# A mixture-of-experts tail: GpSimd's row scatters wait for the next expert's relus, and its DRAINs stand behind experts 3, 6, 9 and 12

## The chip, the cores and the metric

The kernel runs on one core of a Trainium2 chip. The metric is the device time of one execution in microseconds (us), from the first instruction to the last, as the median of several timed runs. Beside the timed runs there is one execution taken by the hardware profiler; its page and trace are what the numbers below come from.

## What is computed

The reference is one transformer block in float32: 8 sequences of 512 tokens with 128 channels. A modulated layer norm feeds attention with 16 heads of 64 channels, whose output is gated and added; then a second modulated layer norm feeds a mixture of 16 experts, and the expert outputs are gated and added again. The change lies in the last part:

```python
score = jax.nn.softmax(xf @ Wg + bg, axis=-1)
gate = jnp.max(score, axis=-1)
idx = jnp.argmax(score, axis=-1)
...
keep = pos < cap                       # cap = 4096 / 16 = 256 rows for each expert
buf = zeros((16, 256, 128)).at[idx, safe_pos].add(where(keep, xf, 0))
h = relu(einsum('ecd,edh->ech', buf, W1) + b1)      # 128 -> 512
y = einsum('ech,ehd->ecd', h, W2) + b2              # 512 -> 128
out = y[idx, safe_pos] * gate
x = x + gb * where(keep, out, 0)
```

## The kernel before

The attention part (8 batches of 8 head pairs, some 780 us of the span) is not touched. At its end GpSimd scatters each token's row (normed input, residual, gate times `gb`, token number: 385 floats) into a DRAM buffer `xbuf` at its expert's place (`scatter`, line 487).

Then the 16 experts follow, each with 256 rows, written out by hand on every engine:

- TensorE, for expert e: `hidden` (line 1270), 12 matmuls into four PSUM banks, three for each bank, with a semaphore step `hm` behind each bank; then the transposes of the next expert's rows (`turn_e`, line 1261); then `down` (line 1295), 16 matmuls that wait bank by bank for the relus (`hr`), with a step `ym` behind each half of 128 rows.
- ScalarE: four relus of 128x256 (line 837), each behind its `hm` and each giving one step of `hr`, which therefore stands at 4(e + 1) when expert e's relus are done. Behind them the high half of the next rows (line 828) and of the weights of the expert after (line 808).
- VectorE: the low halves (lines 1807 and 1773), and `output` (lines 1819 to 1825): token numbers to integers (`yi`), then three operations that add the bias, multiply by the gate and add the residual, with a step of `y` for each half. `output(e - 1)` runs in turn e of the loop up to e = 9 (`LAGGING`); experts 9 to 13 are put out in their own turn, 14 and 15 by halves after the loop.
- SyncE: a load queue; rows of expert e + 5 when `y` says that expert e is out, and weights of expert e + 8 when `ym` says so.
- GpSimd: `expert(e, r)` (line 567): it waits for `yi` and `y`, and starts two indirect DMAs (line 572), a and b below, that write 128 rows each to their tokens' places in the output. The results lie in four buffers `ye`, used in turn, so `output(e)` waits until expert e - 4 has landed (`ysc0` to `ysc3`). A DRAIN stands behind expert 11 and behind the last one (line 580).

The end of the kernel is GpSimd's wait for all four `ysc` semaphores.

Of the kernel before, what the change touches and what calls it, by code (L numbers as in the profile page):

```python
# [44 lines left out]
E, FF = 16, 512  # L45
CAP = B * S // E
NB = FF // P
# [27 lines left out]
def program(nc, x_d, xt_d, wall_d, wv_d, cols_d, wo_d, bo_d, wg_d, bg_d, w1_d, w2_d, b2_d, wmod_d,  # L75
            consts_d, ktab_d, iota_d, out_d):
    ctx = ExitStack()
    with ctx:
# [3 lines left out]
        def sem(name):  # L82
            return ctx.enter_context(nc.semaphore(name))
# [113 lines left out]
        s = {n: sem("s_" + n) for n in names}  # L197
# [177 lines left out]
        def _(gp):  # L375
# [191 lines left out]

            def expert(e, r):
                gp.wait_ge(s["yi"], e + 1)
                for t in range(ST):  # L570
                    gp.wait_ge(s["y"], ST * e + t + 1)
                    gp.indirect_dma_start(out=out_d.rearrange("b s d -> (b s) d"),
                                          out_offset=bass.IndirectOffsetOnAxis(ap=yidx[:, r, t:t + 1], axis=0),
                                          in_=ye[r][:, t, :], in_offset=None,
                                          bounds_check=last_token, oob_is_err=False).then_inc(s[f"ysc{r}"], 16)

            for e in range(E):
                expert(e, e % 4)
                if e in (11, E - 1):
                    gp.drain()  # L580
            for r in range(4):
                gp.wait_ge(s[f"ysc{r}"], 16 * ST * E // 4)
# [1328 lines left out]
```

## Time and profile before

| what | us |
|---|---|
| timed runs: median of 3 | 863.76 |
| timed runs: lowest, highest | 863.61, 4828.07 |
| the profiled execution, its own time | 870.51 |
| its span, first to last instruction | 868.6 |
| TensorE busy (share of the span) | 853.3 (98%) |
| GpSimd busy (share of the span) | 544.7 (63%) |

Stretches and start times below are counted from the span's start. The median stands 6.75 us under the profiled execution's own time. One of the three timed runs took over 4.8 ms; the profile is of an execution without that.

### The profile page before, as it was taken

The page shows a single profiled execution, that of the slowest core. Times are in us where ns is not written, and L with a number is a line of the kernel's source. Part 1 is how long each engine was busy: PE and PEld are TensorE (multiplying, and loading weights), DVE is VectorE, ACT ScalarE, POOL GpSimd, SP SyncE. Part 2 cuts the span into 40 slices and gives each one's busy share as a digit, 9 for nine tenths or more (in the row PEclk, how much of TensorE's full clock was granted, in tenths as well). Part 3 has the DMA queues.
Part 4 walks back from the last instruction along what each step waited for, and adds up shares of the span by engine and source line. Part 5 has one row for each costly group of instructions (what it writes and reads, how often), then busy time and mean ns, then how long its engine had stood idle before and what let it go on. Part 6 is the DMA issues. An engine that isn't in the chain of part 4 may idle for free.

```text
span 868.6 us, 17491 instructions
## 1 busy us (share of the span) xinstructions
PE 853.3 (98%) x5531; PEld 680.2 (78%) x5531; DVE 657.2 (76%) x2041; ACT 724.0 (83%) x2012; POOL 544.7 (63%) x807
## 2 busy tenths in 40 slices
PE   8999999999999999999999999999999999999996
PEld 5777877778877788777787777877778877777985
DVE  6778778777878688777878787877878777876564
ACT  5888888988889888888988889888988888884653
POOL 5856466666576764776567755766667656663454
PEclk9999999999999999999999999999999999999998
DMA  8000970000000100000000000000000000016960
GB/s 295 2 1 2 264 197 14 14 19 20 14 13 1 37 2 13 14 20 18 14 13 9 20 14 13 1 21 2 13 14 13 11 14 13 2 35 191 311 204 23
DMA packets 25611, 41.40 MB, mean 48 GB/s; under 512 B 3334, under 2 KB 17527, under 8 KB 25136
## 3 DMA queue, kind: packets, MB, share of 16 engines
q1 hardware_dynamic: 21872, 33.60, 12.8%
q0 software_dynamic: 3072, 5.94, 1.9%
q8 instruction: 45, 0.74, 0.4%
q10 hardware_dynamic: 576, 0.75, 0.3%
q14 instruction: 46, 0.38, 0.1%
HBM read 25.93 MB, written 16.82 MB: 49 GB/s over the span
## 4 chain that ended last, share of the span: by engine, by line
PE 96%; DVE 2%; ACT 1%; issue 1%; DMA 0%; POOL 0%; POOLq 0%; another core or an unknown queue 0%; DVEq 0%
PE bank L988 23%; PE bank L1021 17%; PE bank L941 17%; PE bank L1001 16%; PE bank L1028 5%; PE bank L968 5%; PE bank L1295 4%; PE bank L985 3%; PE bank L1270 3%; PE bank L961 0%; ACT prob L690 0%; DMA x<-in_x 0%; PE bank L1036 0%; PE bank L891 0%; PE bank L1261 0%
## 5 line engine op out<-in xcount | busy, mean ns | idle before, releaser
L501 POOL TENSOR_SCALAR prob<-prob,rsum 128x128 f32<-128x128 f32 x508 | 261.2, 532 | 220.7 <-DVE rsum L1447 215.5
L690 ACT ACTIVATE prob<-srow,nmax 128x512 f32<-128x512 f32 (+3 forms) x512 | 285.9, 559 | 57.7 <-DVE nmax L1435 56.2
L1435 DVE CUSTOM_DVE_ANT_0 srow<-bank,consts 128x512 f32<-128x512 f32 (+3 forms) x512 | 247.0, 489 | 54.0 <-issue 40.3
L1001 PE MATMUL bank<-consts,prob 128*128 128x128 f32 x1280 | 201.8, 272 | 0.3 <-ACT pt L699 0.3
L1001 PEld LDWEIGHTS bank<-consts,prob 128*128 128x128 f32 x1280 | 158.2, 141 | 23.6 <-ACT pt L699 1.2
L699 ACT ACTIVATE pt<-bank 128x384 f32<-128x384 f32 x318 | 157.0, 498 | 11.3 <-PE bank L1001 11.1
L1452 DVE SCALAR_TENSOR_TENSOR qx<-bank,qbias,consts 128x512 f32<-128x512 f32 x128 | 96.0, 750 | 72.1 <-PE bank L941 65.3
L1021 PE MATMUL bank<-pt,v 128*64 128x512 f32 x1008 | 149.6, 439 | 0.6 <-issue 0.6
L988 PE MATMUL bank<-khi,qhi 128*128 128x512 f32 (+2 forms) x384 | 141.4, 368 | 0.5 <-issue 0.2
L494 POOL TENSOR_TENSOR qlo<-qx,qhi 128x384 fp32r<-128x384 f32 x127 | 128.4, 1011 | 12.4 <-ACT qhi L653 5.7
L988 PE MATMUL bank<-khi,qlo 128*128 128x512 f32 (+2 forms) x384 | 130.3, 339 | 0.0
L988 PE MATMUL bank<-klo,qhi 128*128 128x512 f32 (+2 forms) x384 | 129.0, 336 | 0.0
L1021 PEld LDWEIGHTS bank<-pt,v 128*64 128x64 f32 x1008 | 67.6, 136 | 75.8 <-issue 60.1
L1459 DVE SCALAR_TENSOR_TENSOR klo<-bank,khi 64x512 fp32r<-64x512 f32 x128 | 87.9, 687 | 31.6 <-ACT kx L648 29.5
L690 ACT ACTIVATION_READ_ACCUMULATOR prob<-srow,nmax 128x1 f32 x512 | 97.4, 190 | 0.0
L941 PE MATMUL bank<-hhi,whi 128*128 128x512 f32 x177 | 85.8, 485 | 0.0
L653 ACT ACTIVATE qhi<-qx 128x384 fp32r<-128x384 f32 x128 | 66.3, 518 | 23.3 <-DVE qx L1452 22.0
L988 PEld LDWEIGHTS bank<-khi,qhi 128*128 128x128 f32 x384 | 72.4, 189 | 14.5 <-issue 2.6
L988 PEld LDWEIGHTS bank<-klo,qhi 128*128 128x128 f32 x384 | 72.7, 189 | 10.9 <-issue 0.5
L647 ACT ACTIVATE khi<-bank 64x512 fp32r<-64x512 f32 x128 | 75.1, 587 | 2.1 <-PE bank L908 0.5
L988 PEld LDWEIGHTS bank<-khi,qlo 128*128 128x128 f32 x384 | 72.1, 188 | 5.1
L941 PE MATMUL bank<-hlo,whi 128*128 128x512 f32 x177 | 69.9, 395 | 0.0
(262 smaller groups left out, 1422.8 us busy)
## 6 DMA issues: line engine op xcount, KB each, us to landing
xbuf<-fill SPq DMA_DIRECT2D x4, 1540.0 KB, 23.7
x<-xbuf SPq DMA_DIRECT2D x13, 385.0 KB
raw<-in_w SPq DMA_DIRECT2D x16, 256.0 KB
prob<-in_w SPq DMA_DIRECT2D x16, 256.0 KB
h2T<-in_xt SPq DMA_DIRECT2D x8, 256.0 KB, 2.9
out<-row SPq DMA_DIRECT2D x8, 256.0 KB, 2.4
x<-in_x SPq DMA_DIRECT2D x1, 1536.0 KB, 11.4
modb<-mod_rows SPq DMA_DIRECT2D x1, 1536.0 KB, 7.2
```

The lines of the kernel that those rows point to most:

```text
L494: gp.tensor_tensor(qlo[:, h, :], qx[:, h, P:S], qhi[:, h, :], ALU.subtract).then_inc(s["ql"], 1)
L501: end = gp.tensor_scalar(part, part, rsum[:, par, 4 * h + q:4 * h + q + 1], 1.0, ALU.mult, ALU.mult)
L647: act.activation(khi[0:HD, h, :], source[h * HD:(h + 1) * HD, :], ACT.Copy, scale=C_QKV)
L690: act.activation(prob[:, par, h, QOFF[q]:QOFF[q] + P * (q + 1)], srow[:, k % 4, 0:P * (q + 1)], ACT.Exp, bias=nmax[:, par, k:k + 1], scale ...
L699: act.activation(pt[:, h, KOFF[g]:KOFF[g] + GW[g]], source[:, 0:GW[g]], ACT.Copy)\
L941: last = pe.matmul(out, w[:, a, cols], h, start=(i == 0), stop=(i == 2))
L988: last = pe.matmul(out, a[:, h, (q - 1) * P:q * P], b[:, h, 0:P * (q + 1)], start=(i == 0), stop=(i == 2))
L1001: last = pe.transpose(out[:, n * P:(n + 1) * P], prob[:, par, h, QOFF[q] + k * P:QOFF[q] + (k + 1) * P], ident)
L1021: last = pe.matmul(otb[h * HD:(h + 1) * HD, k * P:S], v[:, g, k, at + h * HD:at + (h + 1) * HD], pt[:, h, KOFF[k]:KOFF[k] + S - k * P], st ...
L1435: dve.tensor_tensor_reduce(out=srow[:, k % 4, 0:w], in0=scb[k % 2][:, 0:w], in1=mask[:, S - w:S], scale=-1.0, scalar=BIG, op0=ALU.add, op1 ...
L1452: dve.scalar_tensor_tensor(qx[:, h, :], prb[h][:, :], qbias[:, h, a:a + 1], qtab, ALU.add, ALU.mult).then_inc(s["qe"], 1)
L1459: dve.scalar_tensor_tensor(klo[0:HD, h, :], source[h * HD:(h + 1) * HD, :], C_QKV, khi[0:HD, h, :], ALU.mult, ALU.subtract).then_inc(s["kl ...
```

## The change

GpSimd waits for one more semaphore value before it scatters expert e, for e from 0 to 13: `hr` at 4(e + 2), which is reached when the four relus of expert e + 1 are done. And the DRAINs, which stood behind experts 11 and 15, stand behind 3, 6, 9, 12 and 15.

```diff
             def expert(e, r):
                 gp.wait_ge(s["yi"], e + 1)
+                if e + 2 < E:
+                    gp.wait_ge(s["hr"], NB * (e + 2))
                 for t in range(ST):
                     gp.wait_ge(s["y"], ST * e + t + 1)
                     gp.indirect_dma_start(out=out_d.rearrange("b s d -> (b s) d"),
...
             for e in range(E):
                 expert(e, e % 4)
-                if e in (11, E - 1):
+                if e in (3, 6, 9, 12, E - 1):
                     gp.drain()
```

No instruction of another engine changes. On GpSimd, at experts 13, 14 and 15 and the end of the program, the order before is (`row` and `xh` hold the results, `yidx` the token numbers; a line's waits are the semaphores it needs):

```order
L572 DMA out<-row,yidx 4096x128 [waits s_y,s_yi]
L572 DMA out<-row,yidx 4096x128 [waits s_y]
L572 DMA out<-xh,yidx 4096x128 [waits s_y,s_yi]
L572 DMA out<-xh,yidx 4096x128 [waits s_y]
L572 DMA out<-xh,yidx 4096x128 [waits s_y,s_yi]
L572 DMA out<-xh,yidx 4096x128 [waits s_y]
L78 UNCONDITIONAL_BRANCH [waits s_ysc2,s_ysc3,s_ysc1,s_ysc0]
```

The same place after the change, where the scatter stands on line 574:

```order
L574 DMA out<-row,yidx 4096x128 [waits s_y,s_hr,s_yi]
L574 DMA out<-row,yidx 4096x128 [waits s_y]
L574 DMA out<-xh,yidx 4096x128 [waits s_y,s_yi]
L574 DMA out<-xh,yidx 4096x128 [waits s_y]
L574 DMA out<-xh,yidx 4096x128 [waits s_y,s_yi]
L574 DMA out<-xh,yidx 4096x128 [waits s_y]
L78 UNCONDITIONAL_BRANCH [waits s_ysc2,s_ysc3,s_ysc1,s_ysc0]
```

Nothing has changed its place; expert 13 is the last with the new wait, and experts 14 and 15 have none. The DRAINs, which such a listing does not print, stand as the diff says.

## Rows read from the trace of the kernel before

**Rows 1.** The page: busy time by engine, and the chain that ended last.

```profile
PE 853.3 (98%) x5531; PEld 680.2 (78%) x5531; DVE 657.2 (76%) x2041; ACT 724.0 (83%) x2012; POOL 544.7 (63%) x807
...
PE 96%; DVE 2%; ACT 1%; issue 1%; DMA 0%; POOL 0%; POOLq 0%; another core or an unknown queue 0%; DVEq 0%
```

**Rows 2.** The chain that ended last, in order of time: start us, us, what.

```profile
852.77 1.42 PE bank L1270 x12
...
856.20 1.42 PE bank L1270 x12
...
860.02 2.34 PE bank L1295 x10
...
862.38 0.30 DVE xh L1822
...
863.33 0.02 issue
863.36 0.02 POOLq L571
863.37 0.73 issue
864.10 0.97 POOL out L572
```

**Rows 3.** Timeline of ACT: start us, us, line, operation, [idle before, releaser].

```profile
836.75 1.57 ACT L837 ACTIVATE srow<-bank,smallT 128x256 f32<-128x256 f32 x4 [1.35 <-PE bank L1270]
...
840.15 0.84 ACT L837 ACTIVATE srow<-bank,smallT 128x256 f32<-128x256 f32 x2 [1.04 <-issue]
841.84 0.47 ACT L837 ACTIVATE srow<-bank,smallT 128x256 f32<-128x256 f32 x1 [0.85 <-PE bank L1270]
843.27 0.47 ACT L837 ACTIVATE srow<-bank,smallT 128x256 f32<-128x256 f32 x1 [0.95 <-remote]
...
849.74 1.57 ACT L837 ACTIVATE srow<-bank,smallT 128x256 f32<-128x256 f32 x4 [1.04 <-PE bank L1270]
...
853.17 1.57 ACT L837 ACTIVATE srow<-bank,smallT 128x256 f32<-128x256 f32 x4 [1.07 <-PE bank L1270]
...
857.25 1.26 ACT L837 ACTIVATE srow<-bank,smallT 128x256 f32<-128x256 f32 x3 [2.24 <-PE bank L1270]
859.49 0.47 ACT L837 ACTIVATE srow<-bank,smallT 128x256 f32<-128x256 f32 x1 [0.98 <-remote]
```

**Rows 4.** Timeline of POOL, scatters of experts 3, 6, 8, 11, 12 and 15.

```profile
820.53 0.97 POOL L572 DMA_INDIRECT out<-xh,yidx  x1 [0.30 <-issue]
822.88 0.97 POOL L572 DMA_INDIRECT out<-row,yidx  x1 [1.38 <-DVE row L1825]
...
831.50 0.97 POOL L572 DMA_INDIRECT out<-xh,yidx  x1 [0.30 <-issue]
...
837.52 0.97 POOL L572 DMA_INDIRECT out<-row,yidx  x1 [1.39 <-DVE yidx L1819]
...
843.90 0.97 POOL L572 DMA_INDIRECT out<-xh,yidx  x1 [0.30 <-issue]
...
849.75 0.97 POOL L572 DMA_INDIRECT out<-xh,yidx  x1 [0.30 <-issue]
853.65 0.97 POOL L572 DMA_INDIRECT out<-row,yidx  x1 [2.92 <-DVE yidx L1819]
...
860.09 0.97 POOL L572 DMA_INDIRECT out<-xh,yidx  x1 [0.30 <-issue]
...
865.37 0.97 POOL L572 DMA_INDIRECT out<-xh,yidx  x1 [0.30 <-issue]
```

**Rows 5.** Timeline of DVE: the last operation of experts 9 and 12.

```profile
838.31 0.42 DVE L1825 TENSOR_TENSOR row<-row,x 128x256 f32<-128x256 f32 x1
...
850.39 0.43 DVE L1825 TENSOR_TENSOR row<-row,x 128x256 f32<-128x256 f32 x1
```

**Rows 6.** Line 580, the DRAINs: count, ns shortest/median/longest.

```profile
L580 POOLq DRAIN  x2: 3621/3871/4121, 848.7 to 864.4; - x2
```

## The prediction

> **What bounds the kernel now.** I read the page first, then the chain that ended last, then the timelines of the engines that the chain passes through. TensorE is busy 98% of the span and makes up 96% of the chain; GpSimd is busy 63%, and the chain knows it only at its end [rows 1]. So most of what GpSimd does is free, and the change touches only the last 60 us of a span of 868.6. There the chain [rows 2] goes through TensorE from expert to expert: the hidden layer of expert 14 starts at 852.77 and that of expert 15 at 856.20, which makes 3.43 us for an expert that nothing delays. The last expert does not keep to that: its second layer is still running at 862.36, VectorE takes the result at 862.38, and GpSimd's wait is over at 863.36, its scatter a begins 0.73 later at 864.10, scatter b at 865.37, and the span ends at 868.6.
>
> By the pace of 3.43 us, expert 15's second layer would be done at 856.20 + 3.43 = 859.63, so it is 2.73 us late. ScalarE's timeline shows where [rows 3]: in experts 10, 13 and 14 the four relus take 1.57 us in one piece, and that of expert 14 starts 0.40 after the hidden layer; in expert 15 they start 1.05 after it (857.25), and the fourth comes after 0.98 us of idle time. Expert 11 shows the same: two relus at 840.15, then gaps of 0.85 and 0.95, so that the fourth starts at 843.27 in place of 840.15 + 1.57 - 0.47 = 841.25, 2.02 late. These are the only two such places among the relus. What they share is seen on GpSimd [rows 4]: both lie in a train of six scatters with 0.30 us between them, 8a to 10b from 837.52 to 843.90 + 0.97 = 844.87, and 12a to 14b from 853.65 to 860.09 + 0.97 = 861.06. Elsewhere the scatters of this part come in pairs with more than 1 us before each pair. That a train holds up TensorE's completions, on which the relus wait, is thus a coincidence of two places, not a thing that a row shows by itself, and the chances below reflect it. The second train exists because of the DRAIN behind expert 11: y of expert 12 was ready at 850.39 + 0.43 = 850.82 [rows 5], but its scatter began at 853.65.
>
> **The change, part by part.** *The new waits.* `output(e - 1)` stands behind `low_x(e + 1)` on VectorE, which needs ScalarE's operation behind the relus of e; so for experts 0 to 8 the new value of `hr` is always there before `y`. For expert 9 it is close: the relus of expert 10 end at 836.75 + 1.57 = 838.32 [rows 3] and y comes at 838.31 + 0.42 = 838.73 [rows 5]. Ten of the fourteen waits cost 0 and move nothing. Expert 10 would wait for the relus of 11, which end at 843.27 + 0.47 = 843.74, but it stands behind a new DRAIN anyway. Expert 12 waits for the relus of 13: 849.74 + 1.57 = 851.31; expert 13 for those of 14: 853.17 + 1.57 = 854.74 [rows 3]. Behind the waiting instruction stand only later scatters; what waits for those is `output(e + 4)` through `ysc`, and the end.
>
> *The DRAINs.* A DRAIN took 3.6 to 4.1 us from its issue [rows 6], but it is issued while the scatters before it still run. Its price on GpSimd is the gap that it makes: from the end of 11b, 849.75 + 0.97 = 850.72, to 12a at 853.65 is 2.93 us, against 0.30 in a train [rows 4], so at most 2.63 each. Below, the bound is 0, where y comes later than the DRAIN ends. I take the whole gap of 2.93, since the one measured case is this very place. By the Trainium skill, Perfetto Trace Analysis, section "DMA Instruction — SWDGE (GPSIMD)", the end that the profiler gives is the point at which the last core has written its descriptors; by that reading alone a DRAIN behind it would have nothing to wait for, expert 15's scatter would not be held by GpSimd at all, and the sum below would gain 2.73 in place of 1.76. The gap of 2.93 does not agree with so short a DRAIN.
>
> The schedule of GpSimd from this, with 1.276 from scatter to scatter ((843.90 - 837.52) / 5, [rows 4]):
> - Behind 3: 3b ends at 820.53 + 0.97 = 821.50, so 4a comes at 824.43 in place of 822.88. It has 1 us and more of slack in each of the next pairs, and is back on time at expert 6. Cost 0.
> - Behind 6: 6b ends at 832.47, so 7a at 835.40, 7b, 8a, 8b, 9a without a break, and 9b at 841.78, ending 842.75. Expert 7 came before in a pair of its own: this is again a train of six, beside the relus of expert 11.
> - Behind 9: 10a at 845.68 in place of 842.62, 10b at 846.96, ending before 11a is due. Here the train of before is cut.
> - 11 as before; no DRAIN, so 12a comes 0.75 behind the relus of 13: 852.06, 12b ends at 854.31.
> - Behind 12: 13a at 857.24, 13b, 14a, 14b at 861.07, ending 862.04; 15a at 862.34, 15b at 863.61.
> Buffers: the scatters of 9 start at latest at 841.78 and those of 10 at 846.96, and VectorE needs their buffers for experts 13 and 14, whose turns come after 851 us; a landing takes at most 868.6 - 865.37 = 3.2 us. Cost 0.
>
> *The sum.* While expert 15's hidden layer and relus run (856.20 to 858.2), GpSimd is now inside the DRAIN for the first half, and the train of four has just begun. I take it that the 2.73 us of delay goes. Then the wait of scatter 15a is over at 863.36 - 2.73 = 860.63, and 15a could start at 861.37; but GpSimd is only free for it at 862.34. What is late next is GpSimd's own queue: 15a moves from 864.10 to 862.34, a gain of 1.76 us, and the rest of the end moves with it. In the middle I count nothing, since the train beside expert 11 is moved and not removed. Span 868.6 - 1.76 = 866.8; own time 870.51 - 1.76 = 868.75. The median of the runs shown stands 6.75 under the profiled time, so 863.76 - 1.76 = 862.0 us.
>
> **The rivals.** *Both stalls go: 860.0.* If what matters is not the length of a train but a scatter that starts beside certain relus, the wait for `hr` cures expert 11 too. For it: 10a moves by 3 us, away from those relus. Against: 8a to 9b stay beside them, only later by 0.43. It would give 2.02 more, 862.0 - 2.0 = 860.0.
>
> *No effect: 863.8.* The stalls do not come from the scatters, or exist only in the profiled execution, which took 6.75 us more than the timed ones. For it: no row names GpSimd as what the relus waited for; two of the gaps have an unknown releaser [rows 3]. Then 15a waits for y at 863.36 as before, and the train ends in time at 862.04. The change would do nothing that it says for ten of fourteen experts anyway.
>
> *Slower: 865.8, by longer trains in front of a late queue.* The place is 7a to 9b: six scatters from 835.40, with a DRAIN at both ends, beside the relus of experts 10 and 11. If a train holds TensorE from its third scatter on, both experts are hit, at 2.02 each where it was one. From then on everything is later by 2.0 us and the end keeps its own stall, since 13a to 14b is still a train of four beside the second layer of expert 15: 863.76 + 2.02 = 865.8. It decides from the point at which a stall shows on the relus of expert 10. Against: before, the first three scatters of each train left the relus alone.
>
> *The median is a disturbed execution.* One timed run took 4828.07 us; were two of three like that, the result would be in milliseconds. No row tells what happened there, and DRAINs could make it rarer or more frequent.
>
> **How the numbers follow.** Forecast, end gain alone: 0.38. Both stalls go: 0.14. No effect: 0.29. Slower by new trains: 0.16. Disturbed median: 0.03. The predicted time is 862.0. The range has to reach to the bounds: at the low side both stalls gone and a little left over, 859.5; at the high side the slower case with 0.2 more for the distance between two medians, 866.0. The two sides leave out the disturbed case and the tails. A difference of 2% is 17 us, about what a measurement of this kernel can tell from no change: all cases but the last lie well within it, and I keep 0.01 for faster and 0.04 for slower.
>
> **What would show it right or wrong.** Right: a gap near 2.9 us on GpSimd behind experts 3, 6, 9 and 12; scatters of 0 to 9 where neither a DRAIN nor a train moves them at the same distance from y; the fourth relu of expert 15 without a gap; 15a directly behind 14b, with an idle time of 0.30, near 862.3. A stall still at the relus of expert 11. Wrong: gaps among the relus of expert 15 with GpSimd inside its DRAIN (then trains are not the cause), a DRAIN that takes 5 us behind three experts' scatters (then 15a is late by itself), or a span that changes in the attention part, which the change does not touch.

## The result, and the profile after

The changed kernel takes 868.57 us (median of 5 runs, 868.28 to 868.72), the kernel before 863.76 beside it. The ratio of the undisturbed runs is 1.0054, with a 95% interval from 1.0041 to 1.0066: slower by 4.8 us, inside 2%, and outside the range of 859.5 to 866.0. The odd part is that the profile says the reverse: its span is 866.7 us after and 868.6 before. Both are true, and how they can be is the main finding of this study.

The page of the changed kernel, as [rows 1]: busy time, then the chain that ended last.

```profile
PE 850.2 (98%) x5531; PEld 678.7 (78%) x5531; DVE 657.1 (76%) x2041; ACT 723.5 (83%) x2012; POOL 545.5 (63%) x807
...
PE 7%; issue 1%; POOL 1%; DVE 0%; POOLq 0%; ACT 0%; DVEq 0%
```

TensorE has hardly changed its share of busy time, but the chain has: before, TensorE made up 96% of it; now the chain can be followed back only to 774.51, and the shares above add up to 9% of the span. Its last stretch, as [rows 2] (start us, us, what):

```profile
852.22 0.30 issue
852.52 0.97 POOL out L574
853.49 0.30 issue
853.80 0.97 POOL out L574
854.77 1.59 issue
856.36 0.04 POOLq L573
856.40 0.73 issue
857.14 0.29 POOL out L574
```

TensorE, ScalarE and VectorE are not in it any more: from 847.42 to the end it is GpSimd's scatters and DRAINs one behind the other. The timeline of GpSimd, as [rows 4]: behind each DRAIN, the end of the scatters before it and the start of those after it, and the last four.

```profile
820.37 0.97 POOL L574 DMA_INDIRECT out<-xh,yidx  x1 [0.30 <-issue]
825.78 0.97 POOL L574 DMA_INDIRECT out<-row,yidx  x1 [4.44 <-ACT srow L839]
...
832.28 1.17 POOL L574 DMA_INDIRECT out<-xh,yidx  x1 [0.30 <-DVE xh L1827]
837.31 0.97 POOL L574 DMA_INDIRECT out<-xh,yidx  x1 [3.86 <-ACT srow L839]
...
844.23 0.97 POOL L574 DMA_INDIRECT out<-row,yidx  x1 [0.30 <-issue]
847.42 0.97 POOL L574 DMA_INDIRECT out<-xh,yidx  x1 [2.21 <-ACT srow L839]
...
853.80 0.97 POOL L574 DMA_INDIRECT out<-row,yidx  x1 [0.30 <-issue]
857.14 0.97 POOL L574 DMA_INDIRECT out<-row,yidx  x1 [2.37 <-DVE xh L1827]
...
859.69 0.97 POOL L574 DMA_INDIRECT out<-xh,yidx  x1 [0.30 <-issue]
860.96 0.97 POOL L574 DMA_INDIRECT out<-xh,yidx  x1 [0.30 <-issue]
862.24 0.97 POOL L574 DMA_INDIRECT out<-xh,yidx  x1 [0.30 <-issue]
863.52 0.97 POOL L574 DMA_INDIRECT out<-xh,yidx  x1 [0.30 <-issue]
```

Four gaps of 4.44, 3.86, 2.21 and 2.37 us stand behind experts 3, 6, 9 and 12; between them the scatters come in full trains, 4a to 6b, 7a to 9b, 10a to 12b and 13a to 15b. Two things are to be read with care. The releaser "ACT srow" is only one of the semaphores that the instruction needs: the DRAINs in front ended at 824.96, 836.49, 846.60 and 856.32, each 0.82 us before the scatter, and e2 below shows that the relus cost nothing. And GpSimd is 63% busy over the whole span, as before, while it has, but for the DRAINs, no free slot in the last 40 us.

The relus of experts 13, 14 and 15 on ScalarE, as [rows 3]:

```profile
845.45 1.57 ACT L839 ACTIVATE srow<-bank,smallT 128x256 f32<-128x256 f32 x4 [1.07 <-PE bank L1272]
...
848.88 1.57 ACT L839 ACTIVATE srow<-bank,smallT 128x256 f32<-128x256 f32 x4 [1.07 <-PE bank L1272]
...
852.30 1.57 ACT L839 ACTIVATE srow<-bank,smallT 128x256 f32<-128x256 f32 x4 [1.59 <-PE bank L1272]
```

They are 3.43 us apart and in one piece, from expert 3 to the last. VectorE is done with expert 15 at 855.99 + 0.29 = 856.28 and the scatters that it feeds start at 862.24, 6 us later. The DRAINs, as [rows 6]:

```profile
L582 POOLq DRAIN  x5: 5608/6618/6948, 819.3 to 859.4; - x5
```

They last 5.6 to 6.9 us from their issue, while the scatters before them still run; what they cost GpSimd is the gap.

### The profile page after: what moved, and what is told of

It reads as the page before. It is cut to its first block and busy times, and to the rows that moved or that the text cites. A ratio compares the mean times of both kernels' runs of the same rounds, so it can differ in the third digit from the quotient of the medians.

```text
span 866.7 us, 17494 instructions
## 1 busy us (share of the span) xinstructions
PE 850.2 (98%) x5531; PEld 678.7 (78%) x5531; DVE 657.1 (76%) x2041; ACT 723.5 (83%) x2012; POOL 545.5 (63%) x807
```

## The experiments

They ran on several chips, and the kernel before, which ran beside each, shows two kinds: on two chips it takes 863.8 to 863.9 us (e1 to e4; e17 and e18), on three others 870.4 to 871.8 us (e5 to e8; e9 to e12; e13 to e16). The two do not overlap: no timed run of it on the first two took over 866.93, none on the other three under 869.62. I call them quiet and stalling. Each chip was used at one time only, so it is not shown whether the difference belongs to the chip or to the time. Every ratio below is against the kernel before on the same chip. The edits shown for e2, e3 and e4 are made to the changed kernel, all others to the kernel before.

**e1: the kernel before again, quiet chip.** No edit.

> The kernel before, unchanged, to see whether its stalls on the relus of experts 11 and 15 are a property of it. Theory Q (the scatter queue of GpSimd is the bound of the changed tail; the profile of before was of an execution with stalls that the timed ones lack): time 863.8, span of the profile near 861.9, each expert 3.43 us apart on ScalarE from expert 3 to 15, no gap among the relus of 11 and 15, the last relus starting near 852.3. Theory S (trains of scatters hold up TensorE, in every run): stalls of 0.9 to 2 us at experts 11 and 15 again, span near 868.6.

Measured: 863.62 us, span 861.4, ratio 0.9996 [0.9986, 1.0006]. Relus of expert 15 and the scatters from 11b on:

```profile
852.09 1.57 ACT L837 ACTIVATE srow<-bank,smallT 128x256 f32<-128x256 f32 x4 [1.58 <-PE bank L1270]
```

```profile
845.29 0.97 POOL L572 DMA_INDIRECT out<-xh,yidx  x1 [0.31 <-issue]
849.18 0.97 POOL L572 DMA_INDIRECT out<-row,yidx  x1 [2.92 <-DVE yidx L1819]
...
856.89 0.97 POOL L572 DMA_INDIRECT out<-xh,yidx  x1 [0.30 <-issue]
858.16 0.97 POOL L572 DMA_INDIRECT out<-xh,yidx  x1 [0.30 <-issue]
```

No stall. The profiled execution that the prediction read (870.51) thus looks like one of a stalling chip, and the timed median beside it (863.76) like one of a quiet chip; that is inferred from the times and the stalls, since their chips are not known. And here the scatter queue sets the end already before the change: the halves of y of expert 15 are ready at 855.17 and 856.06, but 12a to 15b run as one train from 849.18, and 15b starts at 858.16. After the change 15b starts at 863.52, 5.4 later; the spans differ by 866.7 - 861.4 = 5.3.

**e2: the new waits alone (quiet).**

```diff
-                if e in (3, 6, 9, 12, E - 1):
+                if e in (11, E - 1):
```

> The new waits for the relus, the DRAIN left behind expert 11 alone. Theory Q: the waits are met or cost under 0.5 us each on a queue that has slack again, 863.8 to 864.5. Rival W (the waits cost the time, as the profile of after names ScalarE's relus as the releaser of nearly every pair): 866 or more, most of the 4.8 us.

Measured: 864.01, ratio 1.0005 [0.9995, 1.0014]. The waits for the relus cost nothing that these runs can tell, and by the interval at most 1.2 us. Rival W falls, although the profile names the relus for 21.2 us of GpSimd's waits in the changed kernel.

**e3: the DRAINs alone (quiet).**

```diff
-                if e + 2 < E:
-                    gp.wait_ge(s["hr"], NB * (e + 2))
```

> DRAINs behind 3, 6, 9, 12 and 15, without the new waits. Theory Q: all of the 4.8 us, 868.0 to 868.7, with scatters without a break from the one behind 12 to the end. Rival W: 864 to 866.

Measured: 869.47, ratio 1.0059 [1.0045, 1.0073], the same as the change (1.0054). The whole loss is in the DRAINs. One of its six runs took 2169.91 us, so DRAINs behind 3, 6, 9 and 12 do not exclude the long executions.

**e4: the change without its DRAIN behind 12 (quiet).**

```diff
-                if e in (3, 6, 9, 12, E - 1):
+                if e in (3, 6, 9, E - 1):
```

> The change without its DRAIN behind expert 12 (3, 6, 9 and 15 left). Theory Q: the queue is full from 9 on and loses one gap of 2.4 less 0.3, so 2.1 us less than the change: 866.5. If the queue were not the bound: 868.6 as the change.

Measured: 866.98, ratio 1.0033 [1.0022, 1.0045]. It gives back 1.6 of the 4.8 us, against 2.1 expected; in the profile 15b starts at 861.79, 1.73 before that of the change, though its relus of expert 15 come 0.31 later (852.61 against 852.30), which makes 2.04. So the queue part is as expected. Of the rest, 0.3 us is there from the start of the program (TensorE's first output projection begins at 42.38 against 42.09), and 0.25 is in the last DRAIN, which ends 0.53 us behind the last landing in place of 0.28 (see e17).

**e5 and, on other chips, e10, e14 and e17: no DRAIN behind 11.**

```diff
-                if e in (11, E - 1):
+                if e in (E - 1,):
```

> The kernel before without its DRAIN behind expert 11 (15 left). Theory Q, with the schedule of e1: 12a comes at 847.1 in place of 849.2, and the end is bound by y of expert 15 (855.2 + 0.75): 15b near 857.2 in place of 858.16, so 1.0 us less than before: 862.8. If a DRAIN cost only its share of queue time that later slack hides, or the end were not the queue's: 863.8.

> The kernel before without the DRAIN behind expert 11, again. On a chip of the first kind theory Q: 862.8, 1.0 less than before, 15b bound by y. On one of the second kind: 1.7 less than before, as in e5.

> No DRAIN behind expert 11. On a chip without stalls theory Q: 862.8, 1.0 less than before. On one with stalls: 0.6 to 1.7 less, as in e5 and e10.

> No DRAIN behind expert 11. On a chip without stalls theory Q: 862.8, 1.0 less than before. On one with stalls: 0.6 to 1.9 less.

Measured on stalling chips: 868.7, ratio 0.9982 [0.9971, 0.9992] (e5); 871.4, 0.9993 [0.998, 1.0006] (e10); 868.6, 0.9981 [0.9972, 0.9991] (e14). On the quiet chip: 864.24, 1.0002 [0.9993, 1.0012] (e17), where 862.8 was expected: a miss. Its profile, with the relus of expert 15 and the scatters 15a and 15b:

```profile
853.00 1.57 ACT L837 ACTIVATE srow<-bank,smallT 128x256 f32<-128x256 f32 x4 [1.58 <-PE bank L1270]
```

```profile
856.87 0.97 POOL L572 DMA_INDIRECT out<-xh,yidx  x1 [0.66 <-issue]
858.14 0.97 POOL L572 DMA_INDIRECT out<-xh,yidx  x1 [0.30 <-issue]
```

From those relus to 15b it is 5.14 us, against 858.16 - 852.09 = 6.07 in e1: the 0.9 us that the queue theory promised. But the relus themselves come 0.91 later, and so does everything before them. TensorE's first matmul of an output projection, in e1 and then in e17:

```profile
41.83 0.48 PE L1028 MATMUL bank<-ohi,wohi 128*128 128x512 f32 x1
```

```profile
42.76 0.47 PE L1028 MATMUL bank<-ohi,wohi 128*128 128x512 f32 x1
```

The program of e17 is 0.93 late within its first 42 us. That is no fixed property of this kernel: in its profiles on the other chips the same matmul begins at 42.16, 42.42 and 42.08 (e5, e10, e14).

The lateness at the start and the gain in the queue cancel, and 15b starts as in e1 (858.14 and 858.16). Its last increment comes at 860.39, in e1 at 860.41. Yet the span is 862.4 in place of 861.4. That 1.0 us is in the last DRAIN, in e1 and then in e17:

```profile
L580 POOLq DRAIN  x1: 4564/4564/4564, 856.2 to 856.2; - x1
```

```profile
L580 POOLq DRAIN  x1: 4661/4661/4661, 857.1 to 857.1; - x1
```

It ends at 860.77 in e1, 0.36 behind the last landing, and at 861.78 in e17, 1.39 behind it. In e1 the DRAIN behind expert 11 has left eight scatters to it; in e17 it has all 32. So the middle DRAIN, taken out, gives 0.93 us in the queue and takes 1.03 us at the end. That accounts for the miss: the expectation had the first and not the second, and the sum of both, 0.1 us slower, lies within the interval. The gains on the stalling chips are net of the same 1.0 us (1.39 to 1.40 in e5, e10 and e14).

**e6 and, on another chip, e12: the DRAIN behind 12 in place of 11.**

```diff
-                if e in (11, E - 1):
+                if e in (12, E - 1):
```

> The one middle DRAIN behind expert 12 in place of 11, no new waits. Theory Q: 12b ends at 849.3, and 2.37 us of gap put 13a at 851.7, where e1 has it already: 863.8, no change. So a DRAIN's place alone, one expert later, is not what the change pays for. Rival P (the place behind 12 is itself bad): 865 or more.

> DRAIN behind 12 in place of 11 again. On a chip of the first kind theory Q: 13a where it was, no change, 863.8. On one of the second kind: 1.6 less than before, as in e6.

Measured, both on stalling chips: 868.78, ratio 0.9982 [0.9972, 0.9991] (e6), and 869.51, 0.9974 [0.9962, 0.9986] (e12): about 1.7 to 2.3 faster than before. Here 15b starts 0.69 later than in e5 (863.62 against 862.93), and the time is the same, since the last DRAIN ends 0.28 behind the last landing and not 1.40. e6's expectation was written for a quiet chip and was not tested there.

**e7 and, on other chips, e11, e15 and e18: a second DRAIN behind 14.**

```diff
-                if e in (11, E - 1):
+                if e in (11, 14, E - 1):
```

> The kernel before with a second DRAIN, behind expert 14, where the queue has no break any more. Theory Q: one gap of 2.37 less 0.30 is added in full, 2.1 us: 865.9. Rival: a second DRAIN finds the first one's work done and costs under 1 us: below 864.8.

> DRAINs behind 11, 14 and 15 again. On a chip of the first kind theory Q: 2.1 more than before, 865.9, because the queue is the bound there. On one of the second kind: no change, as in e7, where the DRAIN behind 14 lay in front of a late y.

> DRAINs behind 11, 14 and 15. On a chip without stalls theory Q: 865.9, 2.1 more than before. On one with stalls: no change.

> DRAINs behind 11, 14 and 15. On a chip without stalls theory Q: 865.9, 2.1 more than before. On one with stalls: no change.

Measured on stalling chips: ratios 0.9998 [0.9988, 1.0007] (e7), 0.9986 [0.9972, 1.0] (e11), 0.9998 [0.9988, 1.0007] (e15): nothing. On the quiet chip: 865.9, ratio 1.0019 [1.0007, 1.003] (e18), what the queue theory gave; that it agrees to the decimal is luck, for the interval reaches from 0.6 to 2.6 us. In its profile the gap behind 14b is 2.19 us. The same DRAIN costs 2.0 us where the queue is full and nothing where expert 15's y is late anyway.

**e8: no DRAIN at all (stalling).**

```diff
-                if e in (11, E - 1):
-                    gp.drain()
```

> The kernel before without DRAINs behind experts 11 and 15. If a DRAIN returns about 0.3 us after the last scatter has landed (as the trace of after has it, 866.04 against 865.76), the last one costs 0.3 that the wait on the scatters' own semaphores does not: 862.5, 0.3 below e5. If the last DRAIN is hidden under the landing: as e5, 862.8.

Measured: 869.84, ratio 1.0001 [0.9989, 1.0012], where e5 on the same chip has 868.7. Taking out the last DRAIN brought nothing, and what e5 gained is lost. The trace shows where. The program ends with a DRAIN of its own on line 78, in e1 and then in e8:

```profile
L78 POOLq DRAIN  x1: 55/55/55, 861.1 to 861.1; - x1
```

```profile
L78 POOLq DRAIN  x1: 2660/2660/2660, 864.8 to 864.8; - x1
```

In e1 nothing is left to it. In e8 it has all 32 scatters, starts 0.28 behind the last landing (864.57) and ends at 867.51, 2.94 behind it; in e5, whose own DRAIN does that work, it is 1.40. That is 1.5 us more, against 1.1 between the medians. So the expectation's premise, that the wait on the scatters' semaphores could stand in for the DRAIN, failed.

**e13: the scatters of experts 8, 9 and 10 left out (stalling).**

```diff
             def expert(e, r):
                 gp.wait_ge(s["yi"], e + 1)
+                if e in (8, 9, 10):
+                    return
...
-                gp.wait_ge(s[f"ysc{r}"], 16 * ST * E // 4)
+                gp.wait_ge(s[f"ysc{r}"], 32 * (4 - (r < 3)))
...
-                    wait(dve, f"ysc{r}", 32 * (e // 4))
+                    wait(dve, f"ysc{r}", 32 * (e // 4 - (e in (12, 13, 14))))
```

> Leaves out the scatters of experts 8, 9 and 10, so their rows of the output are not written; all else as before. Theory S2 (on the chips with stalls, TensorE is held by trains of scatters): on such a chip the relus of expert 11 come in one piece of 1.57 us and the time falls by about 2 to 3 us, or by what the stall of expert 15 lets through. If the stall stays where it is, scatters are not its cause. On a chip without stalls: queue theory says no change, 863.8, since the queue has caught up with y before expert 12 anyway and the DRAIN behind 11 sets 12a.

Measured: 866.91, ratio 0.9956 [0.994, 0.9973], 3.6 us faster. The relus of expert 11, which came as two, one and one with gaps of 0.85 and 0.95 in [rows 3], and those of expert 15:

```profile
839.92 1.57 ACT L839 ACTIVATE srow<-bank,smallT 128x256 f32<-128x256 f32 x4 [1.05 <-PE bank L1272]
...
854.44 0.47 ACT L839 ACTIVATE srow<-bank,smallT 128x256 f32<-128x256 f32 x1 [2.40 <-PE bank L1272]
855.88 0.47 ACT L839 ACTIVATE srow<-bank,smallT 128x256 f32<-128x256 f32 x1 [0.97 <-PE bank L1272]
857.29 0.84 ACT L839 ACTIVATE srow<-bank,smallT 128x256 f32<-128x256 f32 x2 [0.94 <-remote]
```

The stall beside the train that is gone has gone with it; the one beside 12a to 14b, which is still there, has stayed. So on these chips a train of scatters does hold up what the relus wait for from TensorE. Pairs do it too, by less: without scatters from 836 to 845 the relus of experts 9 to 14 follow each other by 3.41 to 3.43 us, as on a quiet chip, while those of experts 5 to 9 in the same profile take 3.40 to 3.86. The edit takes away GpSimd's issues and the writes together, so it does not tell which of them matters. What e5, e6, e12 and e14 gain has the same face, which is an argument and no test of its own: without the DRAIN behind 11 no train of six stands in front of the relus of expert 15, and they take 1.57 to 1.70 us in one piece, where e7 and e11, with that DRAIN, have them in four and in two pieces. e10, the same kernel as e5 and e14, has them in one piece too (1.74 us) and gained nothing that the interval can tell: its 15a, which waits for y, still comes 5.88 us behind the start of those relus, against 4.41 in e5.

**e9 and e16: the changed kernel again (stalling).** No edit.

> The changed kernel, unchanged, beside the kernel before on the same chip. So far two chips were seen: on one the kernel before takes 863.8 (no stalls of TensorE in the experts), on the other 870.4 (stalls beside trains of scatters). Theory Q: on a chip of the first kind 868.6, 4.8 slower than before, since the queue of scatters is full to the end. On one of the second kind: the last expert's stall lies under the queue, 868.5 to 869, 1.5 to 2 faster than before, as forecast from the profile of such a chip. Rival (the change costs the same anywhere): 4.8 slower on both.

> The changed kernel. On a chip without stalls: 868.6, 4.8 more than before. On one with stalls: within 2 us of before, as in e9.

Measured: 873.18, ratio 1.002 [1.0001, 1.0039] (e9), and 871.04, 1.0007 [0.9998, 1.0017] (e16). Not 1.5 to 2 faster, as e9's expectation had it, but equal or a little slower. Relus of experts 9 and 14 in e16:

```profile
834.51 0.47 ACT L839 ACTIVATE srow<-bank,smallT 128x256 f32<-128x256 f32 x1 [2.48 <-PE bank L1272]
835.90 1.21 ACT L839 ACTIVATE srow<-bank,smallT 128x256 f32<-128x256 f32 x3 [0.92 <-remote]
...
855.59 0.47 ACT L839 ACTIVATE srow<-bank,smallT 128x256 f32<-128x256 f32 x1 [2.77 <-PE bank L1272]
857.00 1.20 ACT L839 ACTIVATE srow<-bank,smallT 128x256 f32<-128x256 f32 x3 [0.94 <-remote]
```

These experts had no such gap before. The DRAINs heap the scatters into trains 4a to 6b, 7a to 9b and 10a to 12b, and on a stalling chip each of them meets the relus of some expert.

## Why the prediction was wrong

**GpSimd's last scatters came where they were put, partly by luck.** 15a was put at 862.34 and 15b at 863.61; the trace has 862.24 and 863.52. 13a: 857.24 against 857.14. The span was given as 866.8 and is 866.7. But the way there was another. The DRAIN behind expert 3 was to cost nothing beyond expert 6; its gap was 4.44 in place of 2.93, and experts 4 to 6 became a train. 9b was put at 841.78 and came at 844.23. Expert 12 was to wait for the relus of 13 and start at 852.06; it started at 852.52 as the fifth of a train from 847.42, on a full queue. The smaller gaps, 2.21 and 2.37 in place of 2.93, made good for it. And the schedule was worked out from the y times of the stalling profile, while the changed kernel ran without stalls. The waits for the relus cost 0 (e2).

**The step that failed is the last line of the sum:** "The median of the runs shown stands 6.75 under the profiled time, so 863.76 - 1.76 = 862.0". It carries a gain found in the profiled execution over to timed runs that were 6.75 us faster. Those 6.75 us were the stalls themselves: e1 has a span of 861.4 without them, 7.2 less. The prediction had found 2.02 and 2.73 of that, at experts 11 and 15, and called 3.43 us the pace of an expert that nothing delays; but its own profile ran slower than that from expert 3 to 10. The relus of expert 3 before, then those of experts 3 and 10 in e1:

```profile
810.88 1.80 ACT L837 ACTIVATE srow<-bank,smallT 128x256 f32<-128x256 f32 x4 [1.07 <-issue]
```

```profile
810.96 1.57 ACT L837 ACTIVATE srow<-bank,smallT 128x256 f32<-128x256 f32 x4 [1.07 <-PE bank L1270]
...
834.95 1.57 ACT L837 ACTIVATE srow<-bank,smallT 128x256 f32<-128x256 f32 x4 [1.07 <-PE bank L1270]
```

To expert 10 (836.75 in [rows 3]) that is 3.70 us for each expert before, and 3.43 in e1. The gain of 1.76 was the queue's end measured against a y of expert 15 that was 2.73 late. In the runs that were timed, that y was not late. There the new schedule of GpSimd, with its end near 863.5, is to be held against 858.16 and not against 865.37. The working needed: take the 6.75 off what stands in front of the queue, and see that the queue then ends the kernel, before the change as after it. 863.52 - 858.16 = 5.4 us slower in the profiled executions, 4.8 in the medians. That the DRAINs make all of it is shown by e2 and e3, and that they do so through a full queue by e4 and e18.

**The rival "no effect" had its premise right and its result wrong.** It said that the stalls might be absent from the timed runs, and gave 863.8, since "15a waits for y at 863.36 as before". But without stalls y of expert 15 is ready by 856.06 (e1), and the queue is late instead. The case without stalls had to be worked out anew and not by leaving out the gain.

**The rival "slower by longer trains"** gave 865.8. The stalling chips show its mechanism (e9, e16: new stalls at experts that had none), with a net loss of 0.6 to 1.4 us, smaller than its 2.0, and not its places: the relus of expert 10 have no gap there, and those of expert 15 come in one piece. It did not decide the result, since the changed kernel's profile has no stall.

**That trains hold up TensorE** was called a coincidence of two places. On a stalling chip it is now shown by e13. On quiet chips it does not happen: the changed kernel has four trains there and all its relus are in one piece, and so have e3 and e4.

**The signs named for right and wrong:** gaps behind 3, 6, 9 and 12, the fourth relu without a gap and 15a directly behind 14b near 862.3 all came true, and the time was still wrong. One sign for right failed: no stall stood at the relus of expert 11 (1.57 us in one piece). That was the sign of the other regime. And one sign for wrong came true by its words, a DRAIN that takes 5 us or more behind three experts' scatters (5.6 to 6.9 from issue), though it did not make 15a later than forecast.

## What to carry to other kernels

When a profiled execution and the timed runs differ by more than the change is worth, the profile is of another regime, and a gain found in its waits may not exist in the runs that count; work the change out for the case in which those waits are absent. A queue that is 63% busy over the span can be full for the last 40 us: count the slots (here 1.276 us for each scatter) from the last place where it had a break to the end. And a DRAIN behind indirect DMAs costs their landing time on such a queue, so it belongs where the queue has a break that it can fill. Leaving it out is not free either: the next DRAIN, or the one that ends the program, takes longer (e17, e8), so count what is left to it.

## What the runs showed of the hardware

- **A GpSimd DRAIN lasts until the scatters before it have landed, and a little longer for each scatter since the DRAIN before.** In the changed kernel the last increments of the scatters' semaphores behind experts 3, 6, 9, 12 and 15 came at 824.59, 836.21, 846.32, 856.04 and 865.76, and the DRAINs ended at 824.96, 836.49, 846.60, 856.32 and 866.04, each 0.28 to 0.37 later. Over the runs that distance goes with the number of scatters since the last DRAIN, by about 0.04 us for each (an estimate from this table):

  | scatters since the last DRAIN | from the last landing to the DRAIN's end, us | for example |
  |---|---|---|
  | 2 | 0.12 | e18, last |
  | 6 | 0.28 | change, behind 12 |
  | 8 | 0.36 | e1, last |
  | 12 | 0.53 | e4, last |
  | 18 | 0.77 | e13, behind 11 |
  | 24 | 1.02 | e1, behind 11 |
  | 26 | 1.10 | e6, behind 12 |
  | 32 | 1.39 | e17, last |

  One of those with six took 0.43 (e11, behind 14). What GpSimd does in that time is not shown.
- **How long the scatters take to land sets the rest.** The gaps of the change differ by it: 3b, issued at 820.37 with the DMA engines 97% busy, took 4.2 us to land, and 12b, issued at 853.80 with them 10% busy, 2.24. The windows are:

```profile
820.00:825.00 5.00, 5.00 (x46) 5.00 (x45) 3.71 (x11) 2.85 (x8) 1.04 (x2) 1.00 0.97 329
...
853.00:857.00 4.00, 2.31 (x19) 2.05 (x18) 1.87 (x7) 0.87 (x3) 1.46 (x2) 1.00 0.10 33
```

  The columns are the stretch, its length, busy time of PE, PEld, DVE, ACT and POOL with counts, granted clock, DMA share and GB/s. The Trainium skill, Perfetto Trace Analysis, section "DMA Instruction — SWDGE (GPSIMD)", puts the profiler's end of such an instruction where the last core has written its descriptors and not where the data has landed. The trace agrees, with records of 0.97 us and landings 2.1 us and more behind the start. What the prediction weighed as following from it, that a DRAIN behind would have nothing to wait for, does not hold.
- **The same kernel ran in two ways on five chips.** On three of them TensorE's completions came late by 1 to 2 us beside trains of scatters, while the granted clock of the profile of before was 1.00 from 836 to 860; on two they did not, with the same program. In the profile of before the last three steps of `hm` for expert 11 came at 840.48, 841.82 and 843.25, in e1 at 838.71, 839.06 and 839.42. TensorE's next weight load (line 1261) began 1.43 us behind the first of the hidden layer in both (840.91 and 839.14). So the matmuls began on time and what reported them came late; where that is held up is not shown. The Trainium skill, SBUF — State Buffer, section "SBUF: two separate sides", says that TensorE's port never waits on anyone; these stalls either have another way in than that port, or speak against it, and no run here tells which.
- The long executions (4828.07, and 2169.91 in e3) were not caught by a profile and stay unexplained.
